# Attention and expert layer on one core: rotated queries and keys stored in the order in which they are placed

## The reference

```python
qkv = layernorm(x) @ w_qkv                       # w_qkv: 256 x 768, 16 heads of 16
q = q * cos + rotate_half(q) * sin               # the same for k
attn = softmax(q @ k.T * 16 ** -0.5)             # for each of 8 batches and 16 heads, 512 x 512
x = x + layernorm(attn @ v @ w_out + b_out)
y = layernorm(x)
shared = (silu(y @ sfc1.T) * (y @ sfc2.T)) @ sfc3.T
moe = sum over the 2 best of 16 experts of weight * silu(y @ w1[e].T) @ w2[e].T
x = x + layernorm(moe + shared)
```

## Time and profile before

| what | value |
|---|---|
| times before, three runs | 910.24, 917.66, 919.96 us (median 917.66) |
| profiled execution, its own time | 915.94 us |
| its span in the profile | 914.1 us |
| TensorE busy | 776.8 us (85% of the span) |
| VectorE / ScalarE / GpSimd busy | 650.4 / 520.9 / 372.9 us |
| DMA | 133.29 MB, mean 146 GB/s |

### The profile page before, as it was taken

The page is one execution under the profiler, slowest core; times in us unless marked ns, Lnnn a source line. Parts: engine busy times, 40 slices in busy tenths (PEclk is TensorE's granted clock), DMA queues, the critical chain, the costliest instruction groups (busy, mean ns, idle before and its releaser), DMA issues. The chain is left out here.

```text
span 914.1 us, 14969 instructions
## 1 busy us (share of the span) xinstructions
PE 776.8 (85%) x4690; PEld 479.2 (52%) x4690; DVE 650.4 (71%) x1256; ACT 520.9 (57%) x1047; POOL 372.9 (41%) x442
## 2 busy tenths in 40 slices
PE   4578798998998989989978877999999788888784
PEld 3433343343443433434422336877877688877673
DVE  4488689688697888887878836778765455553775
ACT  1226577676676777766756754343442466665363
POOL 4430171451630814515300001565665076766442
PEclk9869899898998999989989999999999899999998
DMA  8966637727737568367275401354466355555994
GB/s 157 240 127 167 133 74 157 179 83 163 163 103 170 100 145 179 98 160 163 92 148 88 186 1 52 126 163 150 134 189 210 107 168 172 175 164 193 296 164 92
DMA packets 112421, 133.29 MB, mean 146 GB/s; under 512 B 16724, under 2 KB 80726, under 8 KB 112344
## 3 DMA queue, kind: packets, MB, share of 16 engines
q1 hardware_dynamic: 98616, 108.39, 47.5%
q0 software_dynamic: 13248, 23.15, 9.7%
q10 hardware_dynamic: 480, 0.79, 0.6%
HBM read 68.18 MB, written 59.87 MB: 140 GB/s over the span
## 5 line engine op out<-in xcount | busy, mean ns | idle before, releaser
L480 DVE TENSOR_REDUCE negmax<-ring 128x2 f32<-128x1024 f32 x256 | 306.7, 1212 | 90.4 <-PE ring L643 89.7
L430 ACT ACTIVATE probs<-scores 128x512 f32<-128x512 f32 x498 | 273.6, 599 | 117.3 <-PE scores L661 114.4
L661 PE MATMUL scores<-q_st,k_st 64*128 64x512 f32 x498 | 208.0, 477 | 29.2 <-DMA q_st<-max_rows 16.5
L643 PE MATMUL ring<-k_st,q_st 48*128 48x512 f32 x512 | 187.1, 482 | 26.1 <-issue 9.7
L661 PEld LDWEIGHTS scores<-q_st,k_st 64*128 64x128 f32 x498 | 84.3, 194 | 178.8 <-ACT probs L430 103.1
L675 PE MATMUL av<-probs,v_aug 128*32 128x512 f32 x1024 | 145.0, 640 | 6.3 <-ACT probs L430 6.3
L331 POOL CAST part_r<-negmax 128x16 fp32r<-128x16 f32 x32 | 7.6, 238 | 208.7 <-DVE negmax L480 208.7
L643 PEld LDWEIGHTS ring<-k_st,q_st 48*128 48x128 f32 x512 | 73.3, 199 | 36.7 <-issue 23.1
L166 POOL TENSOR_TENSOR scratch<-qk_raw,cos 128x512 f32<-128x512 f32 x29 | 37.1, 1278 | 82.9 <-ACT qk_raw L383 81.8
L1518 POOL DMA_INDIRECT rows_out<-m_y,projected x48 | 47.3, 985 | 48.1 <-ACT m_y L1583 37.7
L1669 DVE TENSOR_TENSOR m_h_lo<-scores,m_h_hi 128x512 fp32r<-128x512 f32 x40 | 27.6, 691 | 52.2 <-ACT m_h_hi L1569 52.0
(11 more groups left out here) (253 smaller groups left out, 1635.3 us busy)
## 6 DMA issues: line engine op xcount, KB each, us to landing
q_st<-rows_in SPq DMA_DIRECT2D x96, 128.0 KB, 4.5
k_st<-rows_in SPq DMA_DIRECT2D x90, 128.0 KB, 5.5
experts<-split SPq DMA_DIRECT2D x8, 1024.0 KB, 6.0
projected<-records SPq DMA_DIRECT2D x48, 129.0 KB, 2.2
split<-O SPq DMA_DIRECT2D x24, 256.0 KB, 3.0
experts<-rows_out SPq DMA_DIRECT2D x10, 512.0 KB, 8.1
m_rows<-records SPq DMA_DIRECT2D x32, 129.0 KB, 2.4
X<-in_x SPq DMA_DIRECT2D x8, 512.0 KB, 5.0
```

What stands on the lines that cost most here:

```text
L430: nc.scalar.activation(probs[r // 2 % 2][r % 2][:, a, :], score_of(R)[:, a, :], ACT.Exp, scale=HD ** -0.5).then_inc(exp_done, 1)
L480: nc.vector.tensor_reduce(negmax[Gn % 2][:, t, 2 * p:2 * p + 2], ring[t % 2][:, :, :], AX.X, ALU.max, negate=True).then_inc(max_done, 1)
L643: last = nc.tensor.matmul(half[:, a, :], q[rows, t * P:(t + 1) * P], k[rows, :], start=True, stop=True)
L661: nc.tensor.matmul(score_of(R)[:, a, :], k[rows, kt * P:(kt + 1) * P], q[rows, :], start=True, stop=True).then_inc(sc_ps, 1)
```

## The change

The columns of queries and keys are reordered when the projection weights are split, so that after the transposition a half's 64 partitions run over (position in the head, head) and no longer over (head, half, position in the head). To this end the weights' high and low parts are made in three instructions each, and the rotation's patterns have one dimension more. In DRAM a pair and kind now has a region for each half a with its three pieces in order. The store writes each turned tile there: the part that stands twice goes out twice, so three transfers of 256 KB take the place of two, each with 2 x 64 x 512 elements on the DRAM side (the halves lie three pieces apart). The placing is one transfer for each half, 48 partitions by 8 KB, 384 KB each. Before placing, SyncE now also waits until the pair before has been placed. The even pair's queries are placed at the end of turn 0, and not in turn 1 between a store and the maxima. The padding's transfer moves from after group 0 to ahead of the loop. The thresholds of the semaphores follow.

```diff
-    turned = turns[0:4 * N, :].rearrange("(j k c p a) d -> j k c p (a d)", j=2, k=2, c=2, a=2)
+    turned = turns[0:6 * N, :].rearrange("(j k a c x s) d -> j k a c x (s d)", j=2, k=2, a=2, c=3, s=2)
...
+    placed_columns = lambda T, c: T[:, c, 0:2 * D].rearrange("p (k x h) -> p k x h", x=2 * HD, h=GH)
+    weight_pieces = [((lambda T, c=c: placed_columns(T, c)), w_raw[:, c, 0:2 * D].rearrange("p (k h x) -> p k x h", h=GH, x=2 * HD),
+                      placed_columns(w_hi, c).bitcast(F32)) for c in range(DC)]
+    weight_pieces.append((lambda T: T[:, :, 2 * D:3 * D], w_raw[:, :, 2 * D:3 * D], w_hi[:, :, 2 * D:3 * D].bitcast(F32)))
...
-        heads = lambda x: x.rearrange("p (h d) -> p h d", d=HD)
+        heads = lambda x: x.rearrange("p (k d h) -> p k d h", d=HD, h=GH)
...
-        engine.wait_ge(placed[kind], 16 * 6 * (J + 1))
+        engine.wait_ge(placed[kind], 16 * 2 * (J + 1))
...
     def place(engine, J, kind):
-        engine.wait_ge(stored[kind], 32 * (J + 1))
+        engine.wait_ge(stored[kind], 48 * (J + 1))
+        if J > 0:
+            wait_placed(engine, J - 1, kind)
         if J >= 3:
             engine.wait_ge(sc_ps, (J - 3) * 32 + 32)
         st = (q_st, k_st)[kind][J % 3]
-        for off, part in ((0, 0), (16, 1 - kind), (32, kind)):
-            heads = turned[J % 2, kind, part].rearrange("(h a d) n -> a d h n", a=2, d=HD)
-            for a in range(2):
-                engine.dma_start(st[64 * a + off:64 * a + off + HD, :, :].bitcast(F32), heads[a]).then_inc(placed[kind], 16)
+        for a in range(2):
+            engine.dma_start(st[64 * a:64 * a + 48, :, :].bitcast(F32),
+                             turned[J % 2, kind, a].rearrange("c (d h) n -> (c d) (h n)", h=4)).then_inc(placed[kind], 16)
...
         def store(J, kind):
             for part, (src, done) in enumerate(((turned_hi, high_done), (turned_lo, low_done))):
                 sp.wait_ge(done, J * 2 + kind + 1)
-                sp.dma_start(turned[J % 2, kind, part], src[kind][:, :].bitcast(F32)).then_inc(stored[kind], 16)
+                for c in [c for c in range(3) if (0, 1 - kind, kind)[c] == part]:
+                    sp.dma_start(turned[J % 2, kind, :, c], src[kind][:, :].bitcast(F32)).then_inc(stored[kind], 16)
...
-        place(sp, 1, 0)
-        wait_placed(sp, 0, 1)
-        place(sp, 1, 1)
+        for kind in range(2):
+            place(sp, 1, kind)
+        sp.dma_start(rows_in[E * REGION:, :].rearrange("(s p) d -> p s d", p=P), pad[:, :].unsqueeze(1).broadcast_to([P, E, ROW])).then_inc(filled, 16)
         for G in range(-1, NGT):
             turn, b = G % NG, (G + NG) // NG
             if turn == 1 and 1 <= b < B:
                 store(2 * b, 1)
-                place(sp, 2 * b, 0)
...
             if turn == 0 and 1 <= b < B:
                 store(2 * b, 0)
+                place(sp, 2 * b, 0)
...
-            if G == 0:
-                sp.dma_start(rows_in[E * REGION:, :].rearrange("(s p) d -> p s d", p=P), pad[:, :].unsqueeze(1).broadcast_to([P, E, ROW])).then_inc(filled, 16)
...
-        nc.scalar.copy(w_hi[:, :, :], w_raw[:, :, :]).then_inc(w_hi_done, 1)
+        for out, raw, _ in weight_pieces:
+            nc.scalar.copy(out(w_hi), raw).then_inc(w_hi_done, 1)
```

More of the change, by code:

```diff
@@ L160, in number @@
         return Gn * 8 + p * 4 + t
+    placed_columns = lambda T, c: T[:, c, 0:2 * D].rearrange("p (k x h) -> p k x h", x=2 * HD, h=GH)
+    weight_pieces = [((lambda T, c=c: placed_columns(T, c)), w_raw[:, c, 0:2 * D].rearrange("p (k h x) -> p k x h", h=GH, x=2 * HD),
+                      placed_columns(w_hi, c).bitcast(F32)) for c in range(DC)]
+    weight_pieces.append((lambda T: T[:, :, 2 * D:3 * D], w_raw[:, :, 2 * D:3 * D], w_hi[:, :, 2 * D:3 * D].bitcast(F32)))
     def rope_products(engine, t, raw, a, b, done):
-        heads = lambda x: x.rearrange("p (h d) -> p h d", d=HD)
+        heads = lambda x: x.rearrange("p (k d h) -> p k d h", d=HD, h=GH)
         src = heads(raw)
-        c = cos[:, t, :].unsqueeze(1).broadcast_to([P, 2 * H, HD])
-        engine.tensor_tensor(heads(a), src, c, ALU.mult).then_inc(done, 1)
+        table = lambda x: x.unsqueeze(1).unsqueeze(3).broadcast_to([P, 2 * H // GH, x.shape[1], GH])
+        engine.tensor_tensor(heads(a), src, table(cos[:, t, :]), ALU.mult).then_inc(done, 1)
         for half in range(2):
             cols = slice(8 * half, 8 * half + 8)
-            engine.tensor_tensor(heads(b)[:, :, cols], src[:, :, 1 - half::2],
-                                 sin[:, t, cols].unsqueeze(1).broadcast_to([P, 2 * H, 8]), ALU.mult).then_inc(done, 1)
+            engine.tensor_tensor(heads(b)[:, :, cols], src[:, :, 1 - half::2], table(sin[:, t, cols]), ALU.mult).then_inc(done, 1)
     def wait_placed(engine, J, kind):
-        engine.wait_ge(placed[kind], 16 * 6 * (J + 1))
+        engine.wait_ge(placed[kind], 16 * 2 * (J + 1))
     def operands(G, p):
@@ L393, in turned_high @@
             if J > 0:
-                act.wait_ge(stored[kind], 32 * J)
+                act.wait_ge(stored[kind], 48 * J)
             nc.scalar.copy(turned_hi[kind][:, :], bank[:, :]).then_inc(high_done, 1)
@@ L514, in vector_engine @@
         norm_aggregate(0)
-        dve.wait_ge(w_hi_done, 1)
-        nc.vector.tensor_tensor(w_lo[:, :, :], w_raw[:, :, :], w_hi[:, :, :].bitcast(F32),
-                                ALU.subtract).then_inc(w_split, 1)
+        dve.wait_ge(w_hi_done, DC + 1)
+        for out, raw, high in weight_pieces:
+            nc.vector.tensor_tensor(out(w_lo), raw, high, ALU.subtract).then_inc(w_split, 1)
         for t in range(QT):
@@ L677, in attend @@
             last.then_inc(av_ps, 1)
-        pe.wait_ge(w_hi_done, 1)
+        pe.wait_ge(w_hi_done, DC + 1)
         pe.wait_ge(tables, 48)
@@ L683, in job_ahead @@
             if what == "qk" and b == 0 and n == 0:
-                pe.wait_ge(w_split, 1)
+                pe.wait_ge(w_split, DC + 1)
             if what == "xt" and b == 1:
```

## The result

The changed kernel takes 1288.9 us in the median of four runs (1285.1 to 1302.1) against 918.0 us, a ratio of 1.416 (95% interval 1.409 to 1.423): slower by 371 us, where the forecast was 1250. Its profiled execution took 1292.3 us, with a span of 1290.5. One of the executions reported further down, of experiment 4's kernel at 938.8 us, fell in a slow state of the chip, and that kernel's figures rest on its other three.

A forecast was written before the change was run, and what follows sets the result against it. Attention was taken as bound by TensorE, with two-engine stores then chaining each batch to 103 us: 915.94 + 286 for batches + 48.4 at the start + 0.6 for small edits = 1251, said as 1250 us, range 1150 to 1330.

The forecast's parts named there:

- Two engines: Attention's new stores to DRAM: each runs on the same two DMA engines, 5.4 us a store where before 0.7.
- The chain of a batch: Attention batches: stores, placings and maxima wait behind one another in SyncE and its queue; 103 us a batch, +286.
- The start: Before the first scores: stores on two engines, then padding, delay the first maxima; scores at 107.2, not 58.84: +48.4.
- The sum: Whole kernel: 915.94 + 286 + 48.4 + 0.6 = 1251, given as 1250 us.
- Rival 1: Attention's stores run on sixteen engines, maxima and keys come sooner, waits shrink: 881 us; chance 0.11.
- the keys by some 4 us: Step of the sixteen-engine case in attention: the keys go out some 4 us sooner.
- Rival 2: Sixteen engines and no gain, through more bytes written, earlier padding and start traffic: 916 within 9; chance 0.03.
- Rival 3: Attention: two engines but no chain, only the engines' work binds, 83 us a batch: 1111 us; chance 0.04.
- SyncE issues fewer instructions: worth nothing: SyncE's issuing: 18 instructions a pair where before 24, worth nothing while it waits for landings.

The follow-up runs named there:

- experiment 4: The changed kernel with all stores cut into halves of 64 rows and SyncE's order of the kernel before: 928.8 us, 1.020 of the kernel before.

## Why the prediction was right

**Two engines.** Right. The rate in the windows is 51 GB/s; three stores of 256 KB take 15.4 us at it, against the 16.2 assumed.

**The chain of a batch.** Right in every link and a little short in most. The group starts forecast at 38.4, 61.1, 85.0 and 102.9 us came at 41.9, 66.8, 91.4 and 108.2 (from the timeline above, less 239.36). The mis-sized term is what lies between the stores. From the first store's issue to the placing it was 19.4 us for the queries, not 17.8. The queries' placing, two transfers of 384 KB, was taken at 2 us; with the first of the keys' stores behind it, all sixteen engines were busy from about 260.4 to 264.4, at only 197 GB/s:

```profile
260.40:264.40 4.00, 0.00 (x0) 0.00 (x0) 0.00 (x0) 0.00 (x0) 0.00 (x0) 0.50 1.02 197
```

So the keys' stores were alone on their two engines some 5 us after the placing's issue had begun, where the forecast had 2.6. Seven batches gave 750-435 = +315 us, forecast +286.

**The start.** Right in kind, 10 us short: first scores at 117.2 against 107.2. Of this the weights are a part: three strided copies took ScalarE 2.55 us and VectorE 2.57, against 1.47 and, in the trace before, 1.76, so 1.9 us together and not 0.6, and the first store went out at 30.05, not 27.18. By the last placing of the start, issued at 101.22 where the working had its stores landed at 97.5, 4 of the 10 us had come together. The other 6 lie behind it, where that placing and the padding go ahead of the maxima: 16 us to the first scores, forecast 10.

**The sum.** +58.3 at the start and +315 in the batches make 373 of the span's 376 us more; the last four groups have the other 3.

**Rival 1** was rightly given a small chance, but its price, 881 us, was wrong: with sixteen engines and the change's order it is 926 us. Nor do eight engines reach the point where it was to turn into a gain: they give 960. The step that failed in it is "the keys by some 4 us" sooner: I let the queries' placing move forward and didn't charge it to the keys' stores behind it, so that the keys' placing goes out 13.7 to 16.4 us into turn 1, in the kernel before at 12.3 to 13.3. Rival 2 came nearer to what sixteen engines do, though for another reason than the bytes, since the same bytes in the old order give 900. **Rival 3** is refuted by the changed kernel's own trace, in which maxima and placings stand behind the stores and the two engines idle for part of a batch; maxima sent past the stores on their own queue still left 105.6 us a batch, not 83. "SyncE issues fewer instructions: worth nothing" is right only while it waits; on sixteen engines 943 became 926, and 929 became 900, with half the store instructions and longer rows.

## What to carry to other kernels

Ahead of merging transfers, look at the outermost size of both sides of each new one: a layout that makes the read contiguous may leave the write with an outermost size of two, and the share column of a window, 0.13 beside 1.00, is where it is seen; one transfer of that form in the kernel before was enough here to price it. Where both sides can't be contiguous, look whether the order is free: here the contraction's rows could be permuted, which left no side with a small outermost size. And a step moved forward on an in-order engine is charged to everything that it passes: here to the keys' stores, which were on the path while the queries' placing was not.

## What was not expected of the hardware

- While stores on two engines were queued, issuing itself took longer: a low store's issue took 4.12 and 5.43 us and four maxima's 6.97, against 0.33 and 2.70.
- A store of 64 partitions took 0.61 us to issue, one of 128 in the old layout 0.33 and in the interleaved one 0.59 (1.17 for two): the size doesn't set it. What does was not tried.
- GpSimd's rotation became faster with the new patterns, in which the inner runs are of four and the table is repeated along them: 1097 ns against 1278 for the product with cosines and 650 against 747 for that with sines, in the means over the span; VectorE's stayed at 0.69 and 0.41 us. Which of the two did it was not tried.
